# Cross-attention and quantised FFN on one core: first pair of x transposed by VectorE's blocks after a trip through HBM, six layer norms on ScalarE, ctx's second batch asked for first

## What is computed

```python
def xattn(text, features, Wq, bq, Wk, bk):        # text: layer norm of x, features: ctx
    Q = einsum('btx,dx->btd', text, Wq) + bq
    K = einsum('bpx,dx->bpd', features, Wk) + bk
    attn = softmax(einsum('btd,bpd->btp', Q, K) / sqrt(1024))
    return einsum('btp,bpd->btd', attn, features)
def ffn(x, qweight, qzeros, scales, bias, g_idx): # 4-bit weights
    w = where(nibbles(qweight) > 0, 1.0, -1.0)
    return x @ (scales[g_idx] * (w - (nibbles(qzeros) + 1)[g_idx])) + bias
x = x + xattn(layernorm(x), ctx, Wq, bq, Wk, bk)
x = x + ffn(layernorm(x), ...)
```

## Time and profile before

| what | value |
|---|---|
| median of 3 runs | 552.52 us (551.58 to 554.63) |
| profiled execution, own time | 551.12 us |
| its span in the trace | 549.0 us |
| PE busy | 540.2 us, 98% of the span |
| DVE, ACT, POOL busy | 71%, 44%, 34% |
| granted PE clock, mean | 1.00 of full speed |

### The profile page before, as it was taken

How to read it: one execution, slowest core, us unless ns; L and a number is a source line. 1 busy time by engine, 2 the same in 40 slices (tenths; PEclk the granted TensorE clock), 3 DMA queues, 4 the chain that set the end, 5 groups by cost and what they waited for, 6 DMA issues and landing times.

```text
span 549.0 us, 7436 instructions
## 1 busy us (share of the span) xinstructions
PE 540.2 (98%) x2686; PEld 452.6 (82%) x2686; DVE 389.5 (71%) x652; ACT 239.5 (44%) x430; POOL 184.4 (34%) x139
## 2 busy tenths in 40 slices
PE   8999999999999999999999999999999999999997
PEld 7888888787777767778888999998788888888886
DVE  4989775789899996893423555574778789878742
ACT  6973444411432431342437666676462253334210
POOL 1072000010000000000226977777667645744630
PEclk9999999999999999999999999999999999999999
DMA  8942100449687755846374799898436775774311
GB/s 281 300 158 75 38 1 0 150 145 313 203 238 248 205 192 191 244 101 191 117 249 172 287 350 353 326 408 325 175 112 228 213 225 221 229 230 125 105 76 76
DMA packets 56035, 108.13 MB, mean 197 GB/s; under 512 B 12000, under 2 KB 32552, under 8 KB 53824
## 3 DMA queue, kind: packets, MB, share of 16 engines
q1 hardware_dynamic: 49472, 101.38, 53.0%
q10 hardware_dynamic: 6528, 6.29, 5.4%
HBM read 67.74 MB, written 39.85 MB: 196 GB/s over the span
## 4 chain that ended last, share of the span: by engine, by line
PE 77%; DVE 10%; ACT 4%; DMA 4%; issue 2%; POOL 1%; SPq 0%; ACTq 0%; DVEq 0%; POOLq 0%
PE bank L1300 19%; PE bank L1302 19%; PE bank L1301 19%; PE bank L1347 5%; PE bank L1350 5%; PE bank L1353 5%; PE bank L1401 2%; DMA xq<-xn_scratch 2%; DVE xT_lo L895 2%; DMA cin<-in_ctx 1%; DVE xq L998 1%; DMA right_scratch<-part_hi 1%; PE bank L1325 1%; DVE stats L963 1%; DVE part_t L1092 1%
## 5 line engine op out<-in xcount | busy, mean ns | idle before, releaser
L1300 PE MATMUL bank<-xT_hi,m_hi 128*128 128x512 f32 x256 | 101.2, 395 | 1.6 <-DVE xT_lo L895 1.6
L1302 PE MATMUL bank<-xT_hi,m_lo 128*128 128x512 f32 x256 | 99.7, 390 | 0.0
L1301 PE MATMUL bank<-xT_lo,m_hi 128*128 128x512 f32 x256 | 99.6, 389 | 0.0
L787 ACT ACTIVATE t_pair<-bank,ucol 128x512 f32<-128x512 f32 x32 | 22.0, 687 | 100.4 <-PE bank L1302 100.4
L1252 DVE TENSOR_TENSOR xres<-xres,bank 128x512 f32<-128x512 f32 x56 | 38.1, 681 | 35.5 <-PE bank L1302 35.4
L574 POOL TENSOR_TENSOR tT_lo<-t_pair,tT_hi 128x1024 fp32r<-128x1024 f32 x16 | 38.1, 2397 | 73.3 <-ACT tT_hi L616 73.3
L1300 PEld LDWEIGHTS bank<-xT_hi,m_hi 128*128 128x128 f32 x256 | 48.0, 188 | 14.1 <-issue 2.7
L588 POOL TENSOR_TENSOR l_lo_s<-l_sum_s,l_hi_s 128x512 fp32r<-128x512 f32 x32 | 40.4, 1296 | 56.3 <-DVE l_sum_s L1193 56.3
L553 POOL TENSOR_TENSOR pairs<-mv,pairs 128x2 f32<-128x2 f32 x8 | 5.5, 693 | 158.6 <-DVE mv L972 158.6
L1302 PEld LDWEIGHTS bank<-xT_hi,m_lo 128*128 128x128 f32 x256 | 48.1, 188 | 10.1
L1301 PEld LDWEIGHTS bank<-xT_lo,m_hi 128*128 128x128 f32 x256 | 48.1, 188 | 10.0 <-issue 0.2
(11 more groups left out here) (146 smaller groups left out, 1243.5 us busy)
## 6 DMA issues: line engine op xcount, KB each, us to landing
xres<-in_x SPq DMA_DIRECT2D x8, 1024.0 KB, 11.2
out<-xres SPq DMA_DIRECT2D x15, 512.0 KB, 5.0
right_scratch<-part_hi SPq DMA_DIRECT2D x28, 256.0 KB, 2.2
cin<-in_ctx SPq DMA_DIRECT2D x7, 1024.0 KB, 6.4
xn_scratch<-xin SPq DMA_DIRECT2D x6, 1024.0 KB, 5.0
xq<-xn_scratch ACTq DMA_DIRECT2D x24, 256.0 KB, 5.6
r_tile<-right_scratch SPq DMA_DIRECT2D x6, 1024.0 KB, 11.5
yn_scratch<-yin SPq DMA_DIRECT2D x6, 1024.0 KB, 4.0
```

The source lines that it names most:

```text
L1300: pe.matmul(out_, a_hi, b_hi, start=start, stop=False, skip_group_check=True)
L1301: pe.matmul(out_, a_hi, b_lo, start=False, stop=False, skip_group_check=True)
L1302: return pe.matmul(out_, a_lo, b_hi, start=False, stop=stop, skip_group_check=True)
```

## The change

The first pair of x no longer passes through PE. After SP has issued the last load of Wq, it stores batch 0, waits for the store, and reads it back in 32 DMAs of 32 partitions by 8 by 32 elements (128 bytes in one piece, 256 pieces, 32 KB), then the same for batch 1. DVE transposes each batch in blocks (`x_blocks`) in blocks 6 and 7 of the projection, and the eight `x_hi` and `x_lo` split from SBUF, all ahead of `copy_u`. Statistics and apply of batches 0, 1, 4, 5, 6 and 7 go to ACT, as a sum, a negated mean, a sum of squares and an affine copy, with three small POOL instructions each in place of one. The last two `x_lo` of a next pair go ahead of the weight sums. `load_ctx(1)` goes ahead of `load_ctx(0)`.

```diff
-        xq = [None] + [at(f"xq{p}", kb, [P, 2 * NB, S], F32) for p, kb in ((1, slot[2]), (2, slot[4]), (3, 162.25))]
+        xq = [at(f"xq{p}", kb, [P, 2 * NB, S], F32) for p, kb in enumerate((146.25, slot[2], slot[4], 162.25))]
...
+        ON_ACT = {b: i + 1 for i, b in enumerate((0, 1, 4, 5, 6, 7))}
...
+            for b in range(2):
+                store_xn(b)
+                if b == 0:
+                    sp.wait_ge(s_wklo, NB)
+                    sp.wait_ge(s_wkbq, NB)
+                sp.wait_ge(s_xst, 16 * (b + 1))
+                pieces = xn_dram[b].rearrange("(m j) (k a i) -> a m j k i", j=32, a=4, i=32)
+                for a in range(4):
+                    for m in range(NB):
+                        sp.dma_start(xq[0][32 * a:32 * a + 32, NB * b + m, :].rearrange("p (k i) -> p k i", i=32),
+                                     pieces[a, m]).then_inc(s_xq0[b], 16)
             load_raw(2)
...
+            load_ctx(1)
             load_ctx(0)
-            load_ctx(1)
...
+                if n in ON_ACT:
+                    pool.wait_ge(s_xsq, QT * ON_ACT[n])
+                    pool.tensor_scalar(mv[:, :, 1], xsquares, 1.0 / D, EPS, ALU.mult, ALU.add).then_inc(s_xvar, 1)
+                    pool.wait_ge(s_xvar, ON_ACT[n])
...
+            def x_stats(b):
...
+                for t in range(QT):
+                    act.activation(places[t], rows[:, t, :], ACT.Copy, accum_out=xsum[:, t:t + 1]).then_inc(s_xsum, 1)
+                act.wait_ge(s_xsum, QT * ON_ACT[b])
+                act.activation(nmean, xsum, ACT.Copy, scale=-1.0 / D).then_inc(s_xmean, 1)
+                act.wait_ge(s_xmean, ON_ACT[b])
+                for t in range(QT):
+                    act.activation(places[t], rows[:, t, :], ACT.Square, bias=nmean[:, t:t + 1],
+                                   accum_out=xsquares[:, t:t + 1]).then_inc(s_xsq, 1)
+            def x_apply(b):
...
+                    act.activation(out_, in_, ACT.Identity, bias=shift[:, t:t + 1], scale=rstd[:, t:t + 1]).then_inc(s_xn, 1)
...
                     wq_split(b + 1, 0)
+                    if b in (3, 4):
+                        x_stats(b - 3)
                     times_bk(b)
                     wq_split(b + 1, 1)
+                if b in (3, 4):
+                    x_apply(b - 3)
                 if b == NB - 1:
-                    for u in range(6):
+                    for u in range(NB):
                         x_hi(0, u)
...
-                if b in (4, 5):
-                    x_stats(b - 4)
-                    x_apply(b - 4)
+                if b >= NB - 2:
+                    x_blocks(b - (NB - 2))
...
                 if b == NB - 1:
-                    for u in range(5):
+                    for u in range(NB):
                         x_lo(0, u)
                     copy_u()
-                    x_lo(0, 5)
...
+                    if j == NB - 1 and p + 1 < PAIRS:
+                        x_lo(p + 1, NB - 2)
+                        x_lo(p + 1, NB - 1)
                     if n in SUMS:
                         right_sums(SUMS.index(n))
...
-                        for u in {3: (0, 1), 4: (2,), 5: (3, 4), 6: (5,), 7: (6, 7)}.get(c, ()):
-                            x_tr(u)
```

More of the change, by code:

```diff
@@ L156, in xattn_ffn_kernel @@
         junk = at("junk", 200.25, [P, HALF], F32)
+        xjunk = [at(f"xjunk{t}", 188.25 + 2 * t, [P, D], BF16) for t in range(QT)]
+        xjunk_early = [at(f"xjunk_early{t}", 61.75 + 2 * t, [P, D], BF16) for t in range(QT)]
         cn_hi = at("cn_hi", 178.25, [P, QT, D], F32R)
@@ L220, in xattn_ffn_kernel @@
         s_xl = [sem(f"x_loaded{i}") for i in range(2)]
+        s_xsum, s_xmean, s_xsq, s_xvar = sem("x_summed"), sem("x_mean"), sem("x_squares_summed"), sem("x_variance")
         s_stat, s_rstd, s_xn, s_dot = sem("ln_stats"), sem("ln_rstd"), sem("xn_done"), sem("row_terms")
         s_xraw, s_xst = [sem(f"raw_x_loaded{i}") for i in range(2)], sem("xn_stored")
+        s_xq0 = [sem(f"xn{i}_reloaded") for i in range(2)]
         s_xql = [sem(f"xn_reloaded{i}") for i in range(2)]
         s_xT = sem("xn_transposed_by_blocks")
-        s_xtr, s_xhi, s_xlo = sem("xn_transposed"), sem("xT_hi_done"), sem("xT_lo_done")
+        s_xhi, s_xlo = sem("xT_hi_done"), sem("xT_lo_done")
         s_xused = sem("xT_tile_used")
@@ L550, in rsqrt @@
             def rsqrt(n):
[L551 to L552 removed]
+                if n in ON_ACT:
+                    pool.wait_ge(s_xsq, QT * ON_ACT[n])
+                    pool.tensor_scalar(mv[:, :, 1], xsquares, 1.0 / D, EPS, ALU.mult, ALU.add).then_inc(s_xvar, 1)
+                    pool.wait_ge(s_xvar, ON_ACT[n])
+                elif n < B:
+                    pool.wait_ge(s_stat, n - 1)
+                else:
+                    pool.wait_ge(s_stat, n - B + 3)
+                if n in (2, 3):
                     pool.tensor_tensor(rstd, mv[:, :, 1], power, ALU.pow).then_inc(s_rstd, 1)
@@ L669, in _ @@
                 times_bq(c)
+            def x_stats(b):
+                if b < 2:
+                    act.wait_ge(s_xl[b], 16)
+                    rows, places = xin[:, b, :, :], xjunk_early
+                    if b == 0:
+                        act.wait_ge(s_uacc, NB - 1)
+                else:
+                    act.wait_ge(s_xraw[b % 2], 16 * (b // 2))
+                    rows, places = raw_rows(b), xjunk
+                    if b == KH:
+                        act.wait_ge(s_placed, 16 * 8)
+                        act.wait_ge(s_xn, QT * KH)
+                for t in range(QT):
[6 more added lines that the diff above has]
+                                   accum_out=xsquares[:, t:t + 1]).then_inc(s_xsq, 1)
@@ new lines, in x_apply @@
+            def x_apply(b):
+                act.wait_ge(s_rstd, b + 1)
+                if b >= 2:
+                    act.wait_ge(s_xst, 16 * b)
+                    act.wait_ge(s_dot, b)
+                for t in range(QT):
+                    if b < 2:
+                        out_, in_ = xin[:, b, t, :], xin[:, b, t, :]
+                    else:
+                        out_, in_ = by_quadrant(xin[:, 1, t, :]), raw_rows(b)[:, t, :].rearrange("q (k a i) -> q k a i", k=NB, a=4)
+                    act.activation(out_, in_, ACT.Identity, bias=shift[:, t:t + 1], scale=rstd[:, t:t + 1]).then_inc(s_xn, 1)
@@ L671, in x_hi @@
             def x_hi(p, u):
+                act.wait_ge(s_xT, 2 * p + 2)
                 if p == 0:
-                    act.wait_ge(s_xtr, u + 1)
                     act.wait_ge(s_wqused, NB)
-                    copy(xT_hi[:, u, :], bank[6 + u % 2][:, :]).then_inc(s_xhi, 1)
-                else:
[L677 to L683, removed]
+                elif u < NB - 1:
+                    act.wait_ge(s_xused, (NB - 1) * (p - 1) + u + 1)
+                else:
+                    act.wait_ge(s_t, NB * p)
@@ L1001, in x_lo @@
                 dve.wait_ge(s_xhi, NB * p + u + 1)
[L1002 to L1006, removed]
+                low(xT_lo[:, u, :].rearrange("p (m j) -> p m j", j=32), xq[p][:, :, 32 * u:32 * u + 32],
+                    xT_hi[:, u, :].rearrange("p (m j) -> p m j", j=32), s_xlo)
             def copy_u():
@@ L1302, in three @@
                 return pe.matmul(out_, a_lo, b_hi, start=False, stop=stop, skip_group_check=True)
[L1304 to L1311, removed]
             def u_sums():
```

53 lines of the change are left out of this document (24 added, 29 removed).

## The result

| what | before | changed |
|---|---|---|
| median of 5 runs each | 552.28 us (551.21 to 554.63) | 578.28 us (577.47 to 579.47) |
| ratio, 95% interval | | 1.0471 (1.0444 to 1.0498) |
| span of the profiled execution | 549.0 us | 575.7 us |
| PE busy | 540.2 us | 540.4 us |

The kernel is 26 us slower, 4.7%. The forecast was 565.5 us with a range to 575: the sign is right, the size is not, and the result lies 3.3 us outside the range.

What follows compares the result with a forecast made beforehand. PE was taken as the bound, busy 540.2 of 549.0 us. Profiled 551.1 + 13.5 (later `w_row`) + 2.3 (clock) - 1.6 - 1.2 (waits gone) = 564.1; that execution lay 1.4 under the median, so 565.5 us, range 558 to 575.

Steps and rivals of the forecast that it cites:

- When SP is free: SP's list after the last Wq load, delayed by ACT's statistics: first store starts at 64.4 us.
- The chain: Store, reads, store, reads, block transpose, splits, `copy_u`, then `w_row` at 112.6 us instead of 99.1, 13.5 later.
- The issue: SP's 32 reads per batch: 0.45 us each, 14.4 us per batch, with 0.37 and 0.59 as ends.
- The stores: Each batch's store to HBM lands after 4.0 us, upper bound 1.0 more per store.
- The last landing: Batch 1's last read, issued from 100.8 us on, lands 3.5 us later, at 104.3.
- The clock: PE after its long stop at `w_row`: a slow restart costs 2.3 us, lower bound 0.
- What goes away: PE's later waits vanish: 1.6 us for x's low parts in the pairs, 1.2 us for ctx's batch 1.
- Issue hidden behind the transfer: Rival for SP's reads: transfers set the pace; 551.2 us at average rate (chance 0.07), 546.2 at best rate (0.05).
- A new wait in the pairs: Rival: third or fourth pair's splits come one set of ACT statistics late, adding 4.8 us, 570.3 us; chance 0.14.

Runs made afterwards that it cites:

- stores_first: The changed kernel with the second store asked for ahead of batch 0's reads, each store with its own semaphore; single run, 573.54 us.
- few_issues: The changed kernel with each first-pair batch stored in another row order by 4 DMAs and read back in 4 instead of 32; 552.76 us.
- far_steps: The changed kernel with the same 64 reads cut so that the source's inner step is farther than the outer one; 568.41 us.

## Why the prediction was right in sign and short in size

**When SP is free: right.** 64.32 against 64.4. `times_bk` of block 4 ended at 61.22 + 2.44 = 63.7 (forecast 63.8), one set of statistics took 4.7 us (forecast 4.8).

**The chain: right.** Store, reads, store, reads, block transpose, splits, `copy_u`, `w_row`, each released by the one before; stores_first and few_issues moved `w_row` as this chain says. DVE's part was 8.3 us, as forecast.

**The issue: this step failed.** "The nearest is yq on the same queue: also 32 partitions, also 256 pieces out of an HBM scratch ... so I take 0.45". yq was chosen as nearest by its pieces, though the same paragraph sees that issue time does not follow them. What it follows in these reads is whether the source's inner step is shorter or longer than the outer one. By that the nearest row was cin, 0.594, the upper end. Moreover, the length of an issue was taken for the distance to the next, which is 0.05 more. 21.61 + 21.05 us against 2 x 14.4: 13.9 too little. With 0.59 as its length the range's end was too low as well: at a pitch of 0.65 that case comes to 552.5 + 13.5 + 64 x 0.20 + 2.3 - 2.8 = 578.3 us, which is what was measured. That it fits so well is partly luck: the stores, 2.7 too short, are offset by the landing (1.4 too long), the clock (0.6 too dear) and what goes away (0.7 too little).

**The stores: too short by 2.7 in all.** The first took 6.5 (forecast 4.0, bound 5.0), the second 4.2. In far_steps too the first took 6.5 and the second 4.3. SP had issued the last Wq load 0.6 us ahead of the first store, and nothing ahead of the second; that the two collide was not tried by itself.

**The last landing: 1.4 too long.** 2.1 us after its issue (117.1 to 119.2), where 3.5 was taken from cq, whose DMAs are eight times as large.

Together 13.9 + 2.7 - 1.4 = 15.2, against 28.4 - 13.5 = 14.9. Nothing larger is left over.

**The clock: right that it falls, near in price by luck.** 1.7 us against 2.3. The granted clock was 0.50 in 127 to 130 us and 0.92 in the next five. The Trainium skill's page "TensorE: Matmul & The Clock Gate", Part 1, names the same two levels, full speed and half; this trace agrees. But the price was taken from the opening's transposes, and there, from 1.5 to 6.4 us, the profile of the kernel before grants 1.00: what made them slow is not shown to be this clock. And the price varies: measured against the 7.45 us of the kernel before, the restart cost 1.5 us in stores_first, 1.6 in few_issues and 2.6 in far_steps.

**What goes away: right, 0.7 too small.** 2.15 + 1.35 against 1.6 + 1.2. Two reasons were given for the first, the moved `x_lo` and the relief of DVE; moving `x_lo` alone gave 0.3.

**The rivals.** Issue hidden behind the transfer: refuted, 21 us of issue with the DMA engines a third busy. The Trainium skill's page "DMA: Bandwidth & Descriptors", section "Issuing engines are not separate DMA queues", calls the time to start a DMA usually small relative to the DMA; for reads of 32 KB the runs show the contrary, 0.65 us of issue each, and 25.5 us of the kernel's time hung on it. A new wait in the pairs: not there; the delay shrinks in the pairs, from 30.1 to 28.0 us.

## What to carry to other kernels

Price a train of small DMAs by its count times the distance between two issues, from a row whose access pattern has its steps in the same order, and not by bytes or pieces (shown here for reads of 32 partitions); if it is long, permute the rows at the store so that a few DMAs can read them back. A step taken off a saturated engine brings nothing while the new path is longer than the work it runs beside: here the whole change was 4.7% slower with 64 reads and 1.2% faster with 16 DMAs and an earlier copy, of which its later parts alone give 0.7%. And when an instruction is moved ahead in an engine's list, look at who waits for what it passes.

## What the runs showed of the hardware that was not expected

- On SP's queue a read's issue took 0.59 to 0.61 us with the source's inner step shorter than the outer one, and 0.43 to 0.45 with it longer, for 32 partitions and pieces of 128 bytes to 4 KB; one piece a row took 0.42. Order and length of the inner step were not told apart.
- SP and ACT issued trains of 16 beside each other in 10.3 and 10.7 us; SP alone took 10.4.
- After stops of 18.7, 15.2, 13.4, 6.1 and 3.1 us PE came back with a granted clock of 0.50 to 0.55 and took 9.2, 9.0, 10.1, 9.1 and 9.2 us from `w_row` to the first eviction; after a stop of 2.8 us in one execution, and without one, it kept 1.00 and took 7.5. PE had been at work up to each stop.
